# A fused attention-pooling kernel: weighted sums three chunks behind the products instead of two, pooled rows transposed ahead of the next scores

## What is computed

```python
W_b, W_c = (fc1_w[:E], fc1_w[E:])
h = jax.nn.relu(jnp.einsum('bse,eh->bsh', behavior_emb, W_b) + (candidate_emb @ W_c)[:, None, :] + fc1_b)
scores = jnp.einsum('bsh,h->bs', h, fc2_w[:, 0]) + fc2_b[0]
attn = jax.nn.softmax(scores, axis=-1)
user_interest = jnp.einsum('bse,bs->be', behavior_emb, attn)
x = jnp.concatenate([user_interest, candidate_emb], axis=1)
z = jax.nn.relu(x @ mlp1_w + mlp1_b)
logit = (z @ mlp2_w + mlp2_b)[:, 0]
```

## Time and profile before

| | |
|---|---|
| median of 3 runs | 270.85 us (269.1 to 280.69; the runs are 269.1, 270.85, 280.69) |
| the profiled execution | 268.94 us in all, span from first to last instruction 267.2 us |
| GpSimd busy | 43.3 us (16%) |
| queue of the large loads, share of the 16 DMA engines | 93.9% |
| read from HBM | 105.70 MB, 396 GB/s over the span |
| chain that ended last | TensorE 88%, DMA 9%, issue 1%, VectorE 1% |

### The profile page before, as it was taken

How to read it: one execution, slowest core, us unless ns; L and a number is a source line. 1 busy time by engine, 2 the same in 40 slices (tenths; PEclk the granted TensorE clock), 3 DMA queues, 4 the chain that set the end, 5 groups by cost and what they waited for, 6 DMA issues and landing times.

```text
span 267.2 us, 10126 instructions
## 1 busy us (share of the span) xinstructions
PE 262.0 (98%) x3762; PEld 215.1 (81%) x3762; DVE 219.3 (82%) x400; ACT 204.4 (76%) x484; POOL 43.3 (16%) x38
## 2 busy tenths in 40 slices
PE   8999999999999999999999999999999999999995
PEld 7558778888888888888888888888888888888873
DVE  0468988888899988888898888899988888998641
ACT  3567788888889887888888788888888888888402
POOL 2002212110121212012121210112121112212100
PEclk9999999999999999999999999999999999999999
DMA  7999999999999999999999999999999999999600
GB/s 242 425 426 424 420 423 424 426 426 427 427 418 425 427 427 425 429 425 429 429 429 427 422 420 427 427 429 425 425 429 429 427 427 427 420 424 427 274 5 2
DMA packets 10940, 105.87 MB, mean 396 GB/s; under 512 B 1200, under 2 KB 2096, under 8 KB 2992
## 3 DMA queue, kind: packets, MB, share of 16 engines
q1 hardware_dynamic: 10640, 105.51, 93.9%
q10 hardware_dynamic: 288, 0.20, 0.2%
HBM read 105.70 MB, written 0.00 MB: 396 GB/s over the span
## 4 chain that ended last, share of the span: by engine, by line
PE 88%; DMA 9%; issue 1%; DVE 1%; ACT 0%; DVEq 0%; POOL 0%; ACTq 0%; POOLq 0%
PE z_ps L613 18%; PE s_ps L632 16%; PE u_ps L642 16%; PE z_ps L614 15%; PE z_ps L617 15%; DMA xt<-in_behavior_t 9%; PE z_ps L608 2%; PE z_ps L750 1%; PE z_ps L642 1%; PE u_ps L674 1%; PE z_ps L714 1%; PE z_ps L720 1%; DVE hidden L464 0%; ACT xh L329 0%; PE z_ps L700 0%
## 5 line engine op out<-in xcount | busy, mean ns | idle before, releaser
L329 ACT CAST xh<-xt 128x800 fp32r<-128x800 f32 x120 | 101.2, 867 | 26.6 <-DMA xt<-in_behavior_t 24.5
L454 DVE TENSOR_TENSOR xl<-xt,xh 128x800 fp32r<-128x800 f32 x120 | 116.1, 987 | 1.9 <-ACT xh L329 1.6
L371 ACT ACTIVATE hidden<-z_ps,bias 128x200 f32<-128x200 f32 x256 | 88.6, 429 | 16.2 <-PE z_ps L617 13.7
L613 PE MATMUL z_ps<-xh,w_hi 128*128 128x512 f32 x240 | 87.5, 365 | 1.0 <-DVE hidden L464 1.0
L614 PE MATMUL z_ps<-xh,w_lo 128*128 128x512 f32 x240 | 79.5, 346 | 0.0
L296 POOL TENSOR_TENSOR weights_by_row<-weights,masks_sb 128x400 f32<-128x400 f32 x31 | 41.5, 1337 | 208.0 <-ACT weights L336 208.0
L464 DVE TENSOR_TENSOR hidden<-z_ps,neg_bias 128x800 f32<-128x800 f32 x64 | 63.2, 987 | 3.0 <-PE z_ps L608 1.7
L617 PE MATMUL z_ps<-xl,w_hi 128*128 128x512 f32 x240 | 63.1, 344 | 0.0
L613 PEld LDWEIGHTS z_ps<-xh,w_hi 128*128 128x128 f32 x240 | 45.1, 188 | 16.2 <-issue 7.5
L642 PE MATMUL u_ps<-x,weights_by_row 128*32 128x128 f32 x1500 | 50.7, 273 | 0.0
L632 PE MATMUL s_ps<-hidden,f_col 128*3 128x160 f32 (+4 forms) x1280 | 50.3, 301 | 0.0
(11 more groups left out here) (68 smaller groups left out, 81.4 us busy)
## 6 DMA issues: line engine op xcount, KB each, us to landing
x<-in_behavior SPq DMA_DIRECT2D x32, 1600.0 KB, 26.0
xt<-in_behavior_t SPq DMA_DIRECT2D x30, 1600.0 KB, 24.0
xt<-in_behavior_t SPq DMA_DIRECT2D x4, 400.0 KB, 4.9
xt<-in_behavior_t SPq DMA_DIRECT2D x2, 800.0 KB, 8.0
later_sb<-in_later SPq DMA_DIRECT2D x1, 258.5 KB, 22.7
cand<-in_candidate SPq DMA_DIRECT2D x1, 192.0 KB, 5.9
first_sb<-in_first ACTq DMA_DIRECT2D x1, 128.0 KB, 3.9
masks_sb<-in_masks SPq DMA_DIRECT2D x1, 114.0 KB, 4.5
```

What stands on the lines that cost most here:

```text
L329: nc.scalar.copy(xh[g][:, :], xt[q][:, g, :]).then_inc(xh_made, 1)
L371: op = nc.scalar.activation(hidden[q % 2][:, g, :, mine], z[:, :, mine], ACT.Relu, bias=bias[:, bass.ds(c * ROWS + g * EACH + b, 1)])
L454: nc.vector.tensor_tensor(xl[g][:, :], xt[q][:, g, :], xh[g][:, :].bitcast(F32), ALU.subtract).then_inc(xl_made, 1)
L613: nc.tensor.matmul(z[:, a:b], w_hi[:, :], xh[g][:, a:b], start=True, stop=False)
```

## The change

A constant `LAG = 3` replaces the distance of two. The weighted sum of chunk `c-3` (not `c-2`) follows the scores in chunk `c`'s period, so the first one is in chunk 3's period and three are left for the end. The own-layout load of chunk `c-3` (not `c-2`) follows turned load `c`, and the last three own-layout loads come alone at the end. The pair is copied out of `u_ps` in even chunks now; its transpose is done in the next (odd) chunk, ahead of the scores and behind the products of group 1, into the unused columns 800 to 831 of that group's `z` buffer (`beside_z`). ScalarE copies it from there ahead of `hidden` group 1 of the same chunk. The next pair's first sum waits for the first copy alone, not for the second. The periods written out ahead of the loop are seven, not three. At the end the order changes, as the diff shows.

```diff
+LAG = 3
...
-        FIRST = 3
+        FIRST = 7
...
+        def beside_z(q, g):
+
+            return z_view(q, g)[:, WIDTH:WIDTH + 2 * ROWS]
...
             for c in range(2, X_BUFS):
                 load_transposed(c, None)
-                load(c - 2, None)
+            load(0, None)
             sp.dma_start(later_sb[:, :], later).then_inc(later_loaded, 16)
             for c in range(X_BUFS, 2 * X_BUFS):
                 load_transposed(c, c - X_BUFS)
-                load(c - 2, None if c - 2 < X_BUFS else c - 2 - X_BUFS)
+                load(c - LAG, None if c - LAG < X_BUFS else c - LAG - X_BUFS)
...
-                    load(c - 2, (j + 2) % X_BUFS)
-            load(LAST - 1, X_BUFS - 2)
-            load(LAST, X_BUFS - 1)
+                    load(c - LAG, (j - LAG) % X_BUFS)
+            for c in range(CHUNKS - LAG, CHUNKS):
+                load(c, c % X_BUFS)
...
-            def copy_pooled_t(c, bank):
+            def copy_pooled_t(c, summed):
                 act.wait_ge(pooled_t_done, c + 1)
...
                 act.wait_ge(z_done, c * GROUPS + (g + 1))
+                if g == 1 and phase > LAG + 1 and (q - LAG) % 2 == 0:
+                    copy_pooled_t(c - LAG - 1, beside_z(q, g))
...
-                flush = phase >= 2 and (q - 2) % 2 == 1
+
+                flush = phase > LAG and (q - LAG) % 2 == 1
                 biased_relu(c, q, 1, phase)
...
                 if flush:
-                    copy_pooled4(c - 2, u_ps)
+                    copy_pooled4(c - LAG, u_ps)
                 exponents(c - 1, (q + 1) % 2, phase <= 2)
                 next_half(2)
                 biased_relu(c, q, 3, phase)
-                if flush:
-                    copy_pooled_t(c - 2, u_ps)
                 next_half(3)
 
             periods(period)(act)
+            copy_pooled4(LAST - 2, u_ps)
+            copy_pooled_t(LAST - 2, u_ps[:, P:P + 2 * ROWS])
             exponents(LAST, LAST % 2, False)
...
                 elif q % 2 == 0:
 
-                    pe.wait_ge(u_free, c)
+                    pe.wait_ge(pooled4_copied, c)
...
+                    if g == PHASE_AT and phase > LAG + 1 and (q - LAG) % 2 == 0:
+                        transpose_sums(c - LAG - 1, beside_z(q, g))
                     if g == PHASE_AT and phase >= 1:
                         score(c - 1, (q + 1) % 2, phase == 1)
-                    if g == PHASE_AT and phase >= 2:
-                        weighted_sum(c - 2, (q + 2) % X_BUFS, phase == 2)
-                    if g == GROUPS - 1 and phase >= 2 and (q - 2) % 2 == 1:
-                        transpose_sums(c - 2, u_ps)
+                    if g == PHASE_AT and phase >= LAG:
+                        weighted_sum(c - LAG, (q - LAG) % X_BUFS, phase == LAG)
 
             periods(period)(pe)
+            pe.wait_ge(later_loaded, 16)
             row_sums(0)
+            weighted_sum(LAST - 2, (LAST - 2) % X_BUFS, False)
+            score(LAST, LAST % 2, False)
+            transpose_sums(LAST - 2, u_ps[:, P:P + 2 * ROWS])
+            spread_inverses(0)
             weighted_sum_alone(LAST - 1)
-            score(LAST, LAST % 2, False)
-            mlp_candidates(0, 0)
-            spread_inverses(0)
-            mlp_candidates(0, 1)
             mlp_candidates(1, 0)
-            mlp_candidates(1, 1)
             row_sums(1)
             weighted_sum_alone(LAST)
             spread_inverses(1)
-            transpose_sums(LAST, last_pair_ps)
+            mlp_candidates(0, 0)
+            mlp_candidates(0, 1)
+            mlp_candidates(1, 1)
+            transpose_sums(LAST, last_pair_ps[:, P:P + 2 * ROWS])
```

More of the change, by code:

```diff
@@ L187, in attention_pooling_kernel @@
         pooled_t_done = sem("pooled_t_done")
-        u_free = sem("u_free")
+        pooled_t_copied = sem("pooled_t_copied")
         mlp_step = [sem(f"mlp_step{i}") for i in range(2)]
@@ L342, in copy_pooled4 @@
                 nc.scalar.copy(pooled4[:, :], bank[:, 0:P]).then_inc(pooled4_copied, 2)
-            def copy_pooled_t(c, bank):
+            def copy_pooled_t(c, summed):
                 act.wait_ge(pooled_t_done, c + 1)
-                nc.scalar.copy(pooled_t[:, bass.ds((c - 1) * ROWS, 2 * ROWS)],
-                               bank[:, P:P + 2 * ROWS]).then_inc(u_free, 2)
+                nc.scalar.copy(pooled_t[:, bass.ds((c - 1) * ROWS, 2 * ROWS)], summed).then_inc(pooled_t_copied, 2)
             def bias_times_f2(part):
@@ L409, in period @@
                 biased_relu(c, q, 3, phase)
-                if flush:
-                    copy_pooled_t(c - 2, u_ps)
                 next_half(3)
             periods(period)(act)
+            copy_pooled4(LAST - 2, u_ps)
+            copy_pooled_t(LAST - 2, u_ps[:, P:P + 2 * ROWS])
             exponents(LAST, LAST % 2, False)
             copy_pooled4(LAST, last_pair_ps)
-            copy_pooled_t(LAST, last_pair_ps)
+            copy_pooled_t(LAST, last_pair_ps[:, P:P + 2 * ROWS])
             relu(0)
@@ L513, in normalise @@
                 dve.wait_ge(inv_done, part + 1)
-                dve.wait_ge(u_free, b)
+                dve.wait_ge(pooled_t_copied, b)
                 nc.vector.tensor_tensor(pooled_n[:, a * ROWS:b * ROWS], inv[:, 0:(b - a) * ROWS],
@@ L670, in weighted_sum_alone, with transpose_sums @@
                     sum_tiles(c, q, last_pair_ps, LAST_RUN, TILES).then_inc(pooled_done, 1)
-            def transpose_sums(c, bank):
+            def transpose_sums(c, summed):
                 pe.wait_ge(pooled4_copied, c + 1)
-                nc.tensor.matmul(bank[:, P:P + 2 * ROWS], pooled4[:, :], fold, start=True,
+                nc.tensor.matmul(summed, pooled4[:, :], fold, start=True,
                                  stop=True).then_inc(pooled_t_done, 2)
@@ L706, in mlp_candidates @@
                 if part == 0 and m == 0:
-                    pe.wait_ge(later_loaded, 16)
                     pe.wait_ge(hidden_made, CHUNKS * HALF)
@@ L712, in mlp_candidates @@
                 if part == 1 and m == 1:
-                    pe.wait_ge(u_free, LAST - 1)
+                    pe.wait_ge(pooled_t_copied, LAST - 1)
                 nc.tensor.matmul(mlp_ps[part][m][:, 0:b - a], w_mlp[:, 1, m * P:(m + 1) * P], cand_t[:, a:b],
```

## The result

The changed kernel takes 283.99 us (median; 282.01 to 284.81), the kernel before, measured beside it, 269.48 us. The ratio is 1.052, 95% interval 1.047 to 1.057. The profiled execution took 282.01 us, its span is 280.2 us. My forecast was 268.8 us with a range of 266.2 to 271.8, and a chance of 0.04 for slower.

A forecast was written before the change was run, and what follows sets the result against it. TensorE was taken to bound the steady part, with the loads right behind. Span 267.2 + 0.1 (early chunks) + 0 (transposes) - 0.3 (end) = 267.0 us, with 1.74 outside the span 268.8; range 266.2 to 271.8.

The forecast's parts named there:

- the part on chunks 2 to 4: Early chunks: TensorE gets 1.6 us ahead but owes 1.7 of later work, net +0.1 us; ScalarE's wait vanishes without gain.
- My check of chunk 4: Before group 1 of chunk 4: VectorE empties the buffer at 35.9 us, just in time for TensorE at 36.5.
- The loads: Turned chunks 3 to 31 land 3.84 us earlier; the last own-layout load lands as now, with 9 us to spare.
- TensorE's wait before group 1 of chunk 3: TensorE waiting for VectorE's `hidden` early on: grows from 0.8 to 1.8 us, with group 1 starting at 28.8.
- Scores in chunk 4's period: Sign in the chain: these scores stand near 37.7 us, where the kernel before had 39.36.
- The 1.6 us ahead: TensorE's lead at the scores of chunk 4's period, against 1.7 us owed for a sum and a transpose done later.
- The transposes' place: Transposes moved ahead of scores in odd chunks: same number, 0.2 us each as before, so zero change.
- rival 2: Transposes hide whole behind products and handover, 14 x 0.2 = 2.8 us less, giving 266.0 us; chance 0.05.
- rival 4: Each transpose brings a second handover of 0.1 us, 1.4 us more, giving 270.2 us; chance 0.08.
- The end: After scores 31: new filling stays 3.0 us, and candidate products cover the copy before the last transpose; -0.3 us.
- Rival 1: Steady part: loads set the pace and TensorE only follows, so earlier turned loads give 266.5 us; chance 0.13.
- Rival 3: ScalarE becomes the pace: `hidden` of group 1, 0.45 us late in odd chunks, costs 6.3 us, 275.1; chance 0.04.

The follow-up runs named there:

- experiment 1: Changed kernel with one more wait: GpSimd lays out weights only after the first `xl` behind the softmax; 268.15 us, 0.994 of the kernel before.
- the gate at the second `xl`: Changed kernel with GpSimd's layout waiting until the second `xl` behind the softmax is made; 268.34 us, 0.997 of the kernel before.
- both edits: Changed kernel with GpSimd waiting for the first `xl` and `hidden` of group 2 between the two `xl`; 268.05 us, 0.994 of the kernel before.
- experiments 5 and 6: Changed kernel with `hidden` between the two `xl`, 268.12 us; that plus GpSimd waiting for the first `xl`, 268.05; only GpSimd waiting for the second, 268.34.

## Why the prediction was wrong

**What failed** is the sentence on ScalarE's wait in the part on chunks 2 to 4: that it vanishes and "TensorE never paid for it". That TensorE hadn't paid was right. That nothing would change when it goes was not. I asked what waits for ScalarE's `xh`, and not what else stands behind `xh` on ScalarE: the exponential, which releases GpSimd. And I counted no cost between VectorE and GpSimd, although the trace of the kernel before had shown one: 41.5 of GpSimd's 43.3 us are 31 instructions of 1337 ns on average, while the quickest took 872. It was already being held by `xl` for half a microsecond in each chunk; one step of timing earlier and it holds `xl`.

**What it costs.** VectorE's cycle in the changed kernel, from scores at 168.83 to scores at 177.04 us, has scores 1.54, the softmax and its start 1.59, the pair of `xl` 2.48 to `hidden`'s start, `hidden` and its handover 1.11, one group's products 1.35 (a restart), a transpose 0.14: 8.21 us. This is a chunk with a transpose; over all chunks the cycle is 8.16 us. Without the 0.66 us it would be 7.50, 0.16 under TensorE's own 7.66 (experiment 1). So 0.16 of the 0.66 is hidden and 0.5 is paid in each chunk. VectorE's share in the earlier trace rows (82%) looked like room; the cycle through it had almost none. My check of chunk 4 ("just in time", 35.9 against 36.5) had put VectorE 0.6 us ahead, less than one hold of 0.66, and I used it only to see that TensorE wouldn't wait.

**Point by point.** The experiments with GpSimd out of the way test the rest of the sum.
- The loads: turned chunk 3 was there before `xh` wanted it (no wait at 23.58 us), and ScalarE's waits fell to 1.1 us. Right.
- TensorE's wait before group 1 of chunk 3: 1.84 us in the changed kernel (expected 1.8), at 29.11 (expected 28.8). The 1.84 is luck: 0.67 of it is an `xl` already held there. With the gate at the second `xl` the group starts at 28.73 as expected, and TensorE has waited 1.17 us, with 0.27 for an `xl` just before.
- Scores in chunk 4's period: 37.66 us with the gate at the second `xl` (expected near 37.7). The 1.6 us ahead were 1.7. In the changed kernel 38.38, since `xl` had been held twice by then. Scores in chunk 31's period: 244.46 with that gate (expected 245.5), the rest being the transposes.
- The transposes' place: taken as no saving, with rival 2 (hidden) and rival 4 (a second handover) to the sides. It saves 0.07 to 0.08 each, about 1 us, a part of what rival 2 said.
- The end: I took off 0.3 us. From the row sums at 249.86 to the last `logit` at 263.05 the version with the gate at the second `xl` takes 13.19 us; the kernel before takes 264.18 - 252.66 = 11.52 for the same without a sum (1.51) and a transpose (0.2). The gain is 0.0 us. The handover before the last transpose did go (the transpose follows the candidate products without a gap), and as much was lost between the end of scores 31 and sum 31, 253.01 to 256.36 = 3.35 us where it had been 3.02. No wait stands there: the new filling is 0.3 us more work than my estimate of 3.0.
- Rival 1 (the loads set the pace) falls for this change: in experiment 1 TensorE's chunk is 7.66 us while ScalarE waits for turned loads only 1.0 us in the whole run. It isn't far off: with the gate at the second `xl` ScalarE's waits are 10.8 us, with both edits 27.1, and there TensorE's chunk from chunk 13 on is 7.68 us, the pace of the loads. Rival 3 had the right sign and place in the order of things, ScalarE, and the wrong mechanism: ScalarE wasn't late but early. So the 0.04 I gave for slower was no foresight of this.
- Two figures of mine don't follow from their terms: 270.2 us and 0.7% more are 272.1, not 271.8, and rival 3 whole gives 275.1, which is under the 276.3 that I named for slower. Neither bears on the miss.

The sum without the missed term, 267.0 us of span, stands against 266.0 to 266.3 us in the profiles of experiments 5 and 6. The missed term is 0.5 x 27 = 13.5 us against their 7.66 us a chunk, and 280.2 less 266.0 to 266.3 is 14.

## What to carry to other kernels

A wait that the critical engine doesn't feel can still fix the moment at which other engines start. Before removing one, list everything queued behind it and ask under which instruction of which engine each will now fall. Here GpSimd's layout and VectorE's `xl`, with two operands in SBUF, were such a pair; `hidden`, with one in PSUM, was never held. An instruction whose mean is well above its shortest (1337 against 872 ns here) is a sign that they already meet.

Where two cycles run at nearly the same pace, price the margin of the slower engine's cycle (here 0.16 us in 7.66) and not its busy share: a hold of 0.66 us then showed as 5%.

## What the runs showed of the hardware

When VectorE's `xl` and GpSimd's instruction meet, whoever comes first holds the other, and a waiting one goes next, though VectorE has its next `xl` queued: under the first `xl` of the changed kernel GpSimd waited 0.2 us in the early chunks (1.09 us against 0.87 alone) and at most 0.06 later, and the second `xl` then took 0.66 us more. An `xl` holds GpSimd for about 0.85 of its 0.98 us: in the changed kernel GpSimd starts 0.63, 0.79 or 0.81 us after the start of the first `xl` and is each time done 1.72 us after it, its own 0.87 included. The longest single `xl` took 1691 ns, the longest GpSimd layout 1649.

TensorE's wait of 1.2 to 1.8 us ahead of chunk 3's group 1 had a second effect in some runs. In the profile of experiment 1 the granted clock falls right after it (stretches in us, busy us of TensorE, weight loads, VectorE, ScalarE, GpSimd with counts, then the granted clock, DMA share, GB/s):

```profile
30.00:34.00 4.00, 4.00 (x54) 2.63 (x56) 2.28 (x3) 2.26 (x7) 0.00 (x0) 0.59 1.02 432
34.00:38.00 4.00, 4.00 (x67) 3.50 (x56) 3.71 (x9) 2.06 (x5) 1.29 (x1) 1.00 0.99 409
```

0.59 is a mean of the 1.2 and the 2.4 GHz level, and TensorE had stood for 0.55 and 1.17 us shortly before. That execution took 270.28 us, others of the same kernel with the clock at 1.000 took 267.84 and 267.85. The changed kernel's six runs split alike: spans of 282.5 to 283.0 us with a mean clock of 0.993 or 0.994, 280.2 to 280.8 us with 1.000. Where `hidden` comes first and the waits there are shorter, none of eleven runs had less than 0.999. That the wait is the cause is argued from its place only; no run changed it alone, and the profiled execution of the changed kernel has the wait of 1.84 us and a clock of 1.000.
